# The matrix of the read inside a chunk, used from where it is masked: sixteen 32x32 matmuls in place of four 128x128 ones

## The reference, cut to what matters

```
for each token t, sequence b, head h:
    s   = s * alpha[t]                       # state s: 64 x 128, alpha: 64 decays
    u   = k_t . s                            # what the state already holds for the key
    s   = s + beta_t * outer(k_t, v_t - u)   # write
    out = q_t . s                            # read
```

## Time and profile before

| | us |
|---|---|
| median of three runs | 2171.9 |
| the three runs | 2170.96, 2171.9, 2175.56 |
| the profiled execution, its own time | 2175.09 |
| its span, from first to last instruction | 2173.4 |
| TensorE busy in the span | 1553.1 (71%) |
| VectorE busy | 1274.1 (59%) |
| ScalarE busy | 612.4 (28%) |
| GpSimd busy | 368.1 (17%) |
| mean granted TensorE clock | 0.84 of full speed |

### The profile page before, as it was taken

How to read it: one execution, slowest core, us unless ns; L and a number is a source line. 1 busy time by engine, 2 the same in 40 slices (tenths; PEclk the granted TensorE clock), 3 DMA queues, 4 the chain that set the end, 5 groups by cost and what they waited for, 6 DMA issues and landing times. The chain is left out here.

```text
span 2173.4 us, 43513 instructions
## 1 busy us (share of the span) xinstructions
PE 1553.1 (71%) x16904; PEld 955.8 (44%) x16904; DVE 1274.1 (59%) x3384; ACT 612.4 (28%) x1224; POOL 368.1 (17%) x513
## 2 busy tenths in 40 slices
PE   1248977887797788778778878877894676564551
PEld 0023654464365446435543643554362353334551
DVE  1748656865865685586567558655552545454445
ACT  2041234124123412422341242133022323332221
POOL 2110131013012201301220130032010112111005
PEclk9577987997898799789979987997896867778995
DMA  1351101100110010011001001100104000001112
GB/s 52 121 189 30 31 11 31 22 9 12 30 31 7 26 30 12 12 30 28 9 17 39 11 12 30 26 6 12 44 11 139 15 15 28 16 10 31 37 32 80
DMA packets 160304, 72.63 MB, mean 33 GB/s; under 512 B 129505, under 2 KB 141089, under 8 KB 160098
## 3 DMA queue, kind: packets, MB, share of 16 engines
q1 hardware_dynamic: 148962, 46.66, 8.6%
q10 hardware_dynamic: 8448, 16.78, 2.1%
q0 software_dynamic: 2688, 6.30, 1.0%
HBM read 31.49 MB, written 38.21 MB: 32 GB/s over the span
## 5 line engine op out<-in xcount | busy, mean ns | idle before, releaser
L455 POOL COPY kx<-kend_t 32x256 f32<-32x256 f32 x256 | 114.5, 447 | 896.3 <-PE ps L909 853.7
L855 PE MATMUL ps<-wv,ident 128*128 128x512 f32 x480 | 231.1, 631 | 37.3 <-DVEq L1208 37.2
L1267 DVE SCALAR_TENSOR_TENSOR state<-state,gam,ps 128x128 f32<-128x128 f32 x512 | 137.5, 341 | 74.2 <-PE ps L909 74.2
L855 PEld LDWEIGHTS ps<-wv,ident 128*128 128x128 f32 x480 | 92.1, 199 | 174.7 <-issue 153.4
L1223 DVE TENSOR_TENSOR nv<-ps,nrm 128x512 f32<-128x512 f32 x64 | 44.2, 691 | 209.6 <-PE ps L797 209.0
L1090 DVE TENSOR_TENSOR kq_leaf<-kq,eleaf 128x1024 f32<-128x1024 f32 x32 | 40.4, 1264 | 156.5 <-ACT dleaf L562 107.2
L909 PE MATMUL ps<-w,kx 128*64 128x128 f32 x2048 | 128.8, 280 | 0.0
L909 PEld LDWEIGHTS ps<-w,kx 128*64 128x64 f32 x2048 | 113.4, 139 | 13.0 <-issue 13.0
L1195 DVE TENSOR_TENSOR tmp<-kq,kq_blk 128x31 f32<-128x31 f32 (+15 forms) x248 | 114.5, 462 | 1.3
L813 PE MATMUL ps<-yt,wout 128*128 128x128 f32 x512 | 89.2, 346 | 26.4 <-ACT yt L542 26.4
L720 PE MATMUL ps<-yt,headind 128*16 128x512 f32 x128 | 85.9, 809 | 29.9 <-ACT yt L535 29.9
(11 more groups left out here) (268 smaller groups left out, 3273.8 us busy)
## 6 DMA issues: line engine op xcount, KB each, us to landing
slot_d<-zeros ACTq DMA_DIRECT2D x16, 1024.0 KB, 13.1
b_d<-ab SPq DMA_DIRECT2D x32, 128.0 KB, 2.0
a_d<-kq_pair SPq DMA_DIRECT2D x8, 512.0 KB, 2.6
kq_blk<-a_d SPq DMA_DIRECT2D x32, 128.0 KB, 2.9
u_d<-kq SPq DMA_DIRECT2D x8, 512.0 KB, 2.6
ub<-u_d SPq DMA_DIRECT2D x128, 32.0 KB, 1.9
bb<-b_d SPq DMA_DIRECT2D x128, 32.0 KB, 1.9
wall<-in_w SPq DMA_DIRECT2D x8, 512.0 KB, 7.3
```

The source lines that it names most:

```text
L455: m = pool.tensor_copy(kx[part, :, b4, :], kend_t[part, g, 2 * q:2 * q + 2, :])
L855: pe.matmul(bd[k % 2].t[:, :], ident[:, :], wv[:, 0:512], start=True, stop=True)
L1267: k = dve.scalar_tensor_tensor(out=state[:, hp, b, :], in0=state[:, hp, b, :], scalar=gam[:, hp, b:b + 1], in1=bd[j].t[:, DV * x:DV * x + ...
```

## The change

B is no longer stored to DRAM and loaded as padded blocks. TensorE takes it out of `ab`, with one 32x32 stationary matrix for each sequence and head: sixteen matmuls for a tile, 32 partitions to 32 output partitions, 128 columns each, in place of four of 128 partitions to 128. The four of one head lie on the diagonal of the array: partitions 32*b4 in, partitions 32*b4 out. `bb`, `b_d`, their memset, their 20 DMAs a chunk and their semaphores are gone, and so is VectorE's wait for the store before it masks the next chunk. The sum that is computed is the same but for the zeros.

```diff
@@ SyncE, body @@
-            sp_e.wait_ge(ab_ready.sem, ab_ready.at(c, 1))
-            settle(c)
-            if later(c):
-                for j in range(2):
-                    sp_e.wait_ge(bb_loaded[j].sem, bb_loaded[j].at(c, 128, 1))
-            for g in range(NG):
-                sp_e.dma_start(b_d[:, :, g, :, :].rearrange("b j (a h) i -> (b j) a (h i)", h=2),
-                               ab[:, :, 1, 2 * g:2 * g + 2, :].rearrange("p a h i -> p a (h i)")
-                               ).then_inc(b_stored.sem, 16)
...
             sp_e.wait_ge(tri_done.sem, tri_done.at(c, 1))
+            settle(c)
...
-            sp_e.wait_ge(b_stored.sem, b_stored.at(c, 16 * NG))
...
-                for buf, dram, loaded in ((ub, u_d, ub_loaded), (bb, b_d, bb_loaded)):
-                    for b4 in range(GB):
-                        rows, cols = slice(CH * b4, CH * b4 + CH), slice(CH * b4, CH * b4 + CH)
-                        src = dram[b4, g].rearrange("h c i -> c h i") if dram is u_d else dram[b4, :, g]
-                        sp_e.dma_start(buf[rows, g % 2, :, cols], src).then_inc(loaded[g % 2].sem, 16)
+                for b4 in range(GB):
+                    rows, cols = slice(CH * b4, CH * b4 + CH), slice(CH * b4, CH * b4 + CH)
+                    sp_e.dma_start(ub[rows, g % 2, :, cols],
+                                   u_d[b4, g].rearrange("h c i -> c h i")).then_inc(ub_loaded[g % 2].sem, 16)
@@ GpSimd @@
-        pool.memset(bb[:, :, :, :], 0.0).then_inc(s_zero, 1)
@@ TensorE, body, tile i @@
                     pe.wait_ge(bw.drained.sem, bw.emptied(c, f"w{i}"))
-                    if q == 0:
-                        pe.wait_ge(bb_loaded[g % 2].sem, bb_loaded[g % 2].at(c, 64 * (g // 2) + 64))
                     pe.wait_ge(by.drained.sem, by.freed(c, f"y{i}"))
                     settle(c)
                     for hq in range(4):
-                        cols = slice(DV * hq, DV * hq + DV)
-                        m = pe.matmul(by.t[:, cols], bb[:, g % 2, 4 * q + hq, :], w[:, hq, :], start=(hq == 0),
-                                      stop=False)
+                        hp, h2, cols = 2 * q + hq // 2, hq % 2, slice(DV * hq, DV * hq + DV)
+                        for b4 in range(GB):
+                            part = slice(CH * b4, CH * b4 + CH)
+                            m = pe.matmul(by.t[part, cols], ab[part, hp, 1, 2 * g + h2, :], w[part, hq, :],
+                                          start=(hq == 0), stop=False)
                     m.then_inc(row_step, runs.next())
                     pe.wait_ge(row_step, runs.n)
@@ VectorE, mask_leaves @@
-            if p == 0 and later(c):
-                dve.wait_ge(b_stored.sem, b_stored.at(c, 16 * NG, 1))
```

More of the change, by code:

```diff
@@ L154, in attention @@
     a_d = nc.dram_tensor("a_d", (GB, CH, UN, CH), F32, kind="Internal").ap()
-    b_d = nc.dram_tensor("b_d", (GB, CH, NG, H, CH), F32, kind="Internal").ap()
     u_d = nc.dram_tensor("u_d", (GB, NG, H, CH, CH), F32, kind="Internal").ap()
@@ L217, in attention @@
     state = sb("state", [P, HP, NB, DV])
-    ub, bb = sb("ub", [P, 2, 8, P]), sb("bb", [P, 2, 8, P])
+    ub = sb("ub", [P, 2, 8, P])
     nv, r, w = sb("nv", [P, 4, DV]), sb("r", [P, 4, DV]), sb("w", [P, 4, DV])
@@ L272, in attention @@
     ab_ready, ca_step = sig("ab_ready", 1), sig("ca_step", 2)
-    a_stored, b_stored, na_loaded = sig("a_stored", 16), sig("b_stored", 16 * NG), sig("na_loaded", 64)
+    a_stored, na_loaded = sig("a_stored", 16), sig("na_loaded", 64)
     tu_cleared, tri_step, tri_done = sig("tu_cleared", 1), sem("tri_step"), sig("tri_done", 1)
@@ L276, in attention @@
     ub_loaded = [sig(f"ub_loaded{j}", 128) for j in range(2)]
-    bb_loaded = [sig(f"bb_loaded{j}", 128) for j in range(2)]
     yss_ready, ylog, yrs_ready = sig("yss_ready", NG), sig("ylog", NG), sig("yrs_ready", NG)
@@ L296, in attention @@
     n_const, n_late = 16 * len(loads), 16 * len(late_loads)
-    n_made = 18
+    n_made = 17
     def quad(t, g, q):
```

## The result

| | before | after |
|---|---|---|
| median of the runs (range, count) | 2173.73 us (2170.96 to 2176.5, 4) | 2209.4 us (2208.22 to 2216.33, 4) |
| ratio, 95% interval | | 1.0171 [1.0145, 1.0197] |
| span of the profiled execution | 2173.4 us | 2207.9 us |
| mean granted TensorE clock | 0.840 | 0.832 |

The account below looks back on a forecast made before the run. TensorE's program was taken as the path in the tiles, with 57 slots on it. Gains of 3.3 us from the slots and 0.65 from the loads made -3.9 us, 2168.0 us from the median; range 2161 to 2186.

Parts of the forecast that it names:

- The slot: TensorE's B w matmuls in a tile: 1.22 to 1.16 us at full clock, 2.13 to 2.04 at half; 3.3 us less.
- entry: TensorE's wait ahead of the B w matmuls in a tile: the same 0.20 us, bound 3 us either way.
- loads: SyncE's loads of B: the 0.65 us idle ahead of chunk 0's first B w matmul goes, once; bounds 0 and 5.
- store: B's store ahead of the solve: removing it gives 0, with 2.5 us of slack; bound 16 us of gain.
- idle ahead of tile 6: TensorE's wait in tile 6 for VectorE's scan of the next chunk's decays: 1.91 us, to get a touch longer.
- lifetime of `ab`: TensorE reads `ab` until tile 7; VectorE's older wait for y of tile 7 covers it, so no wait is added.
- memset: GpSimd's clearing of `bb` at the start goes; GpSimd sits idle 17.69 us there, so it gives nothing.
- rival A: B w matmuls in the tiles: row groups don't run side by side; 2321 us, or 2218 two at a time; chance 0.13.
- C: B w matmuls in the tiles: no gain, they stay at 1.22 us, only 0.65 us is left, 2171.2 us; chance 0.12.
- rival D: TensorE's clock: a small shift moves where its falls come, either sign; runs 4.6 us apart; chance within the forecast's 0.60.
- Issue is no limit: B w matmuls in a tile: issuing 32 instructions at 0.023 us takes 0.74 us, under the 0.86 of streaming.
- Rival B: TensorE's clock in the tiles falls as 32x32 matmuls use a quarter of the array; 2179 to 2201 us; chance 0.15.

Follow-up runs that it names:

- experiment 4: One matmul of pure delay per chunk, in tile 1; on the kernel before, 0.43 us gave 2204.59 us (1.0108) and 0.13 us gave 2188.07 us (1.0076).
- experiment 6: Changed kernel with the matmuls that bridge the solve's waits written as four diagonal 32x32 tiles: 2181.69 us, 1.0019 to the kernel before.
- late start: Changed kernel with 1.7 us of matmul added once, in tile 1 of chunk 0 alone: 2208.13 us, 1.0136 to the kernel before.

## Why the prediction was wrong

- **The slot, entry, loads, store:** right. 1.16 and 2.02 us; the entry 0.20; the 0.65 us went; solve -0.2; idle ahead of tile 6 is 1.97 for 1.91. For the lifetime of `ab` and the memset nothing speaks against the zeros. Rivals A and C are out: the four row groups work side by side, and the slot did get shorter.
- **The step that failed** is the price of rival D: "Luck of the clock, either sign: the runs before lie 4.6 us apart, about one long fall; a shift of a tenth of a us a tile moves where it comes." I saw that a small shift moves the stretches and then priced it as one draw, within the forecast's own range. The runs show it in six of seven chunks, +18.4 us net. That what moves in one moves in nearly all, because all chunks run the same code, is my reading of it. The runs with pure delay show the lever, 1.0 us of work for 16.5.
- **Missing from the sum** is the code itself. Under "Issue is no limit" I counted 0.023 us an instruction and never asked where 384 more instructions per chunk (half of them weight loads) put the places at which TensorE stops. That is the products' part, 14.7 us in six stages. The second stop accounts for 10.3 of it, as the stages with and without it show, and the table of places shows that the stops go by the length of the code ahead of them. That a stop is the wait for the packet is argued from its timing, not shown by itself. The 5.8 us between the second and third block are not traced to a cause.
- **Rival B** had the sign and, with 2201 as its upper end, the nearest size. Its mechanism is not what the runs show: halves on all 128 rows lose as much within the intervals, 32x32 matmuls held the clock in the solve, and the old form loses by delay alone. What the earlier trace rows do show is the same mix, as busy, at either level.
- **Open:** what in the changed kernel sets off the six stretches, the stops (which shift VectorE's and TensorE's work against each other) or the 0.06 us a slot. That is more than half of the loss. Delay alone can set them off (experiment 4, old kernel), and without the stops they were gone at a slot of 1.16 (experiment 6); the two together point at the stops, in one kernel only. Against them, the late start has the stops in all six stages and the stretch in four of seven chunks.

## What to carry to other kernels

A looped kernel repeats its accidents: price a move of the clock by the number of turns, not as one draw, and control for it with a delay of a tenth of a us before believing a small change. Fill TensorE's short idle times first, here worth 27 us where the change sought 4. Splitting a matmul into many small ones lengthens the code: look under "issue" in rows of tiny matmuls and where the instruction queue's packets fall, and see whether the idle time moves when a few instructions are added ahead of the loop.

## What was unexpected of the hardware

- Four diagonal 32x32 tiles that write four quarters of one bank stream side by side: 32 instructions in 1.07 us. The rule that rival A takes from the Trainium skill, read strictly, gave a slot of 3.76; measured 1.16.
- TensorE stopped for up to 2.2 us in the midst of a block of small matmuls and went on 2.2 to 2.9 us after a 16 KB instruction packet began, in all 156 cases. The place moved by two instructions for each matmul added ahead of the loop.
- Idle time of 1.9 us could be followed by nothing or by some 10.2 us at 1.2 GHz, from turn to turn of the same code: one in seven before, six in seven after.
